# A two-layer decoder on one core: passes of the identity at stage ends and in front of the expert lists

## The chip, the cores and the metric

The kernel runs on one core of a Trainium2 chip. The metric is the device time of one execution in microseconds; lower is better. The program is one launch. Its engines are TensorE (PE; its weight loads are shown as PEld), VectorE (DVE), ScalarE (ACT), GpSimd (POOL) and SyncE (SP), which mainly issues DMA transfers.

## What is computed

The reference is a decoder of two layers over 8 sequences of 112 tokens with width 512, and a context of 375 tokens per sequence:

```
x += self_attention_0(layernorm(x))          # 16 heads, tril mask times scores
x += cross_attention_0(layernorm(x), ctx)    # 16 heads, int8 fake quantisation
x += ffn_0(layernorm(x))                     # rms, rope attention (32 query, 8 kv heads of 64),
                                             # rms, top 4 of 16 experts: (silu(h w1) * (h w3)) w2
x += self_attention_1(layernorm(x))          # 16 heads, low-rank additions to each projection
x += joint_attention_1(layernorm(x), ctx)    # 16 query heads, 4 kv heads of 128, rope
x += experts_1(layernorm(x))                 # top 6 of 16 experts, plus shared ones
```

All data are float32.

## The kernel before, in words

The program is a row of twelve stages, each with its own semaphores and PSUM tile of eight banks: front, self0, cross1, p2, self2, r2c4, the expert stage e2, self3, p4, joint4, s5 and the expert stage e5. At the end of each, `Stage.__exit__` frees its semaphores and puts a barrier of all engines (lines L82 and L84). Each engine drains, reports, and goes on when all have; the slowest engine sets the time.

Most stages are a `Segment`. It holds parts (a projection, an attention, an output product), and each part has one program per engine, written as a generator. `run(order)` walks a hand-made list of part names on every engine, and so sets in which order the parts' steps stand in each queue (`play`). The parts that matter here:

- `ContextPart` in front makes keys and values of the context. It multiplies into banks 0 to 3 for keys and 4 to 6 for values (L133), and DVE evacuates them (L2870, L2874). Its semaphore k_ready counts the evacuated key blocks, 4 per batch.
- `SelfAttentionPart` makes scores (L1498), a softmax on DVE, POOL and ACT (L1527, L1531, L1474, L1565), transposes (L1487, L1670 in the cross attention) and products with the values (L1511). `CrossAttentionPart` has scores at L1682 and value products at L1695. These operands are plain float32; scores of one head use 32, 64 or 128 rows.
- Most projections (L133, L1362) split each operand into a high and a low float32r part and multiply three times.
- `RopeQkvPart` in p2 and p4 makes queries, keys and values in banks 0 to 5.

`routed_expert_stage` (e2 and e5) works through a list of items of 128 token rows for one expert. For an item, DVE makes a one-hot matrix (L856), PE turns it into a list of tokens (L910, L912), DVE forms indices (L835, L839), POOL gathers the rows from DRAM by an indirect DMA (L734), PE transposes them (L920), ACT and DVE split them (L778, L844), and PE multiplies by the expert's weights (L876 to L878). The result is weighted, transposed (L886; L942 at the end), multiplied again and added to DRAM by POOL (L745). All engines read table words into registers first (L677, L596). The weights of the first expert are loaded in the stage before; ACT and DVE split them (L760, L807, L813). In DVE's queue the first list's index steps stand ahead of the split L807.

Line L82 is where the profile puts the drains of a stage end. The identity, `core.ident`, is a float32 tile of 128 x 128 that the transposes use too.

Of the kernel before, what the change touches and what calls it, by code (L numbers as in the profile page):

```python
# [63 lines left out]
class Stage:  # L64
# [36 lines left out]

    def block(self):
        return self.ctx.enter_context(self.nc.Block()) if self.shared is None else self.shared.block


class Order:
# [495 lines left out]
def routed_expert_stage(core, name, routing, w_up, w_down, chunks, h_rows, acc, raw, next_raw=()):  # L602
# [6 lines left out]
    with Stage(core, name) as s:  # L609
# [259 lines left out]

        @block.tensor  # L870
        def _(pe):
            pe.wait_ge(made, n_made)

            def split_product(out, lhs, rhs, k, n_k):

                pe.matmul(out, lhs[0], rhs[0], start=k == 0, stop=False)  # L876
                pe.matmul(out, lhs[0], rhs[1], start=False, stop=False)  # L877
                return pe.matmul(out, lhs[1], rhs[0], start=False, stop=k == n_k - 1)  # L878

            def tick(j, u, item, now):  # L880
                i = item(-1)
                if i is not None:
                    pe.wait_ge(act_ready, i + 1)
                    reuse(pe, a_ready, i)
                    for c in range(n_c):
                        last = pe.transpose(ps[0:chunks[c], A_BANK, c * 128:(c + 1) * 128], act_raw[:, offs[c]:offs[c] + chunks[c]],  # L886
                                            core.ident[:, :])
                    last.then_inc(a_transposed, 1)
                i = item(0)
                if i is not None:  # L890
                    e, which = now.e, now.which
                    slot = e % 2
                    pe.wait_ge(h_ready, i + 1)
                    reuse(pe, act_ready, i - 1)

                    with pe.If(which != TT):
                        for k in range(KC):
                            pe.wait_ge(up_ready, e * KC + k + 1)
                            for part in range(2):
                                cols = slice(part * hid, (part + 1) * hid)  # L900
                                last = split_product(ps[:, 2 * (u % 2) + part, 0:hid], (hT[0][u % 2][:, k, :], hT[1][u % 2][:, k, :]),
                                                     [w[:, bass.ds(slot * KC + k, 1), cols] for w in (up_hi, up_lo)], k, KC)
                        last.then_inc(gu_done, 1)
                    with pe.If(which == TT):
                        pe.matmul(ps[:, 2 * (u % 2), 0:2], hT[1][u % 2][:, 0, :], hT[1][u % 2][:, 0, 0:2], start=True, stop=True).then_inc(gu_done, 1)
                i = item(2)
                if i is not None:
                    pe.wait_ge(onehot_ready, i + 1)
                    reuse(pe, idx_ready, i)
                    pe.matmul(ps[:, LIST_BANK, 0:3], id_bf[:, :], spare_no[:, :], start=True, stop=False)  # L910
                    for m in range(TT):
                        last = pe.matmul(ps[:, LIST_BANK, 0:3], onehot[:, u % 2, m, :], token_no[:, m, :], start=False, stop=m == TT - 1)  # L912
                    last.then_inc(listed, 1)
                i = item(1)
                if i is not None:
                    v = (u + 1) % 4
                    pe.wait_ge(gathered[v % 2], landed(i, v % 2))
                    reuse(pe, h_ready, i)
                    for c in range(KC):
                        last = pe.transpose(ps[:, H_BANK, c * 128:(c + 1) * 128], rows[:, v, c * 128:(c + 1) * 128], core.ident[:, :])  # L920
                    last.then_inc(h_transposed, 1)
                i = item(-1)
                if i is not None:
                    e, which = now.e_before, now.which_before
                    slot = e % 2
                    pe.wait_ge(a_ready, i + 1)
                    reuse(pe, y_ready, i)

                    with pe.If(which != TT):
                        pe.wait_ge(dn_ready, (e + 1) * n_dn)  # L930
                        for k in range(n_c):
                            last = split_product(ps[:, Y_BANK, :], [t[0:chunks[k], k, :] for t in aT],
                                                 [w[0:chunks[k], bass.ds(slot * n_c + k, 1), :] for w in (dn_hi, dn_lo)], k, n_c)
                        last.then_inc(y_done, 1)
                    with pe.If(which == TT):
                        pe.matmul(ps[:, Y_BANK, 0:2], aT[0][:, 0, :], aT[0][:, 0, 0:2], start=True, stop=True).then_inc(y_done, 1)
            n_used = run(pe, tick)
            j = n_used // 2 * 2
            pe.wait_ge(act_ready, j + 2)
            pe.wait_ge(a_ready, j + 1)  # L940
            for c in range(n_c):
                last = pe.transpose(ps[0:chunks[c], A_BANK, c * 128:(c + 1) * 128], act_raw[:, offs[c]:offs[c] + chunks[c]], core.ident[:, :])  # L942
            last.then_inc(a_transposed, 1)


class Segment(Stage):
# [18 lines left out]
            for _ in rest:  # L965
                pass

    def run(self, order):
        block = self.ctx.enter_context(self.nc.Block())

        @block.sync
        def _(sp):
            self.play(sp, "sync", order)

        @block.gpsimd
        def _(pool):
            self.play(pool, "gpsimd", order)

        @block.vector
        def _(dve):  # L980
            self.play(dve, "vector", order)

        @block.scalar
        def _(act):
            self.play(act, "scalar", order)

        @block.tensor
        def _(pe):
            self.play(pe, "tensor", order)


class RopeQkvPart:
# [1753 lines left out]
class ContextPart:  # L2746


    def __init__(self, g, name, wk, wv, k_to, v_to, biases, k_banks, v_banks):
# [15 lines left out]
        c_ready = g.sems(f"{name}_c_ready", 2)  # L2765
        b_in, first_c_in, hi_ready, c_hi_ready, padded, k_mm, v_mm, k_ready, v_ready = (
            g.sem(f"{name}_{n}") for n in ("b_in", "first_c_in", "hi_ready", "c_hi_ready", "padded", "k_mm", "v_mm", "k_ready", "v_ready"))
        self.steps = 1 + B * KC

        def values(b, n):  # L2770

# [331 lines left out]
def decoder(nc, ins, out, blocks=range(6), debug_x=None):  # L3103

    with ExitStack() as ctx:
# [24 lines left out]
        if True:  # L3130
            with ExitStack() as held:
                wq = held.enter_context(nc.sbuf_tensor("x0_wq", [128, KC, D], F32R))
                q_scale = held.enter_context(nc.sbuf_tensor("x0_q_scale", [128, KC], F32))
                with Segment(core, "front") as g:
                    c = ContextPart(g, "c1", "L0_xattn_wk", "L0_xattn_wv", k_ctx, v_ctx, ("L0_xattn_bk", "L0_xattn_bv"),
                                    k_banks=(0, 1, 2, 3), v_banks=(4, 5, 6))
                    n = FirstNormPart(g, "n0", (7,), late=1)
                    w, wq_tmp = c.w_raw[:, 0, :, :], c.w_raw[:, 1, :, :]
                    first = QuantWeightPart(g, "w1q", "L0_xattn_wq", w, wq_tmp, lambda sp: sp.wait_ge(c.w_ready[0], KC),
                                            lambda dve: dve.wait_ge(c.w_ready[1], KC), wq, 7,  # L3140
                                            lambda pe: pe.wait_ge(n.t_free, B), scale=q_scale)
                    second = QuantWeightPart(g, "w1p", "L0_xattn_wp", w, wq_tmp, lambda sp: sp.wait_ge(first.wq_ready, KC),
                                             lambda dve: dve.wait_ge(first.t_done, KC), wp_hi, 7,
                                             lambda pe: pe.wait_ge(first.done, KC), lo=wp_lo)
                    order = ["c1", "n0"] + ["c1"] * 4 + ["c1", "n0"] * (n.steps - 1)
                    order += ["w1q"] + ["c1", "w1q", "w1q"] * 7 + ["w1p"] + ["c1", "w1p", "w1p"] * 5 + ["c1", "w1p"] * 5
                    f = FirstWeightPart(g, "f", ins["L0_attn_Wq"], first_hi, first_lo)
                    g.run(order[:24] + ["f"] + order[24:-30] + [n for name in order[-30:-25] for n in (name, "f")] + order[-25:])
                others = held.enter_context(nc.sbuf_tensor("x1_others", [128, 4, KC, D], F32R))
                flat = others[:, :, :, :].bitcast(F32).rearrange("p a k d -> p (a k d)")  # L3150
                n_q, n_k, n_v = 2 * 4 * T, 2 * 4 * C, 2 * CCH * (D + 96)
# [3 lines left out]
                with Segment(core, "self0") as g:  # L3155
# [11 lines left out]
                    order = ["x"] + self_attention_order(p, a, o, then.steps)  # L3167
                    keys_at = len(order) - order[::-1].index("p") + 4
                    queries_at = [i for i, n in enumerate(order) if n == "then"][5]
                    g.run(order[:keys_at] + ["x"] + order[keys_at:queries_at] + ["x"] + order[queries_at:])  # L3170
                with Segment(core, "cross1") as g:
                    a = CrossAttentionPart(g, "a", 32, lambda b: q1[b], lambda b: [(slice(0, C), k_ctx[b])],
                                           lambda b: [v_ctx[b, c, 0:CT, :] for c in range(CCH)], [CT] * CCH, 32.0 ** -0.5,
# [7 lines left out]
        with hold_h0:  # L3181
            with ExitStack() as inner:
                cos_t = inner.enter_context(nc.sbuf_tensor("f0_cos", [128, TT, 2, 32], F32))
                sin_t = inner.enter_context(nc.sbuf_tensor("f0_sin", [128, TT, 2, 32], F32))
                with Segment(core, "p2") as g:
# [9 lines left out]
                        [(v2[:, 0, 0:8 * 65].rearrange("p (h e) -> p h e", e=65)[:, :, 0:64], v_all[tokens_of(0), :].rearrange("t (h d) -> t h d", d=64))]],  # L3195
                        ones=v2)
                    order = ["p"] * 4 + ["p", "t", "t"] * (t.steps // 2)
                    g.run(f.placed(order + ["t"] * (t.steps - order.count("t")) + ["p"] * (p.steps - order.count("p"))))
            with Segment(core, "self2") as g:
                wo = [g.sb(f"wo_{part}", [128, 16, D], F32R) for part in ("hi", "lo")]  # L3200
                a = SelfAttentionPart(g, "a", *own_qkv(64, 32, 0.125, (0, 1), (2, 3), (4, 5), "causal", ALU.add), tiles=(q2, k2, v2))
# [42 lines left out]
        if 4 in blocks:  # L3244
# [4 lines left out]
            with Segment(core, "p4") as g:  # L3249
# [7 lines left out]
                    [(k4[:, 0, :, C:C + T], k_all[:, tokens_of(0)].rearrange("(c p) t -> p c t", p=128))] +  # L3257
                    [(v4[0:CT, 0, c, :], v_ctx[0, c, 0:CT, :]) for c in range(CCH)],
                    [(v4[0:T, 0, CCH, :], v_all[tokens_of(0), :])]])
                g.run(f.placed(["p"] * p.steps))  # L3260
            with Segment(core, "joint4") as g:
                wo = [g.sb(f"wo_{part}", [128, 16, D], F32R) for part in ("hi", "lo")]
                a = CrossAttentionPart(g, "a", 128, lambda b: q_all[:, tokens_of(b)],
# [117 lines left out]
```

## Time and profile before

| | us |
|---|---|
| median of 3 runs (lowest, highest) | 2848.71 (2846.34, 2851.26) |
| the profiled execution, own time | 2851.77 |
| its span, first to last instruction | 2850.1 |
| PE busy in the span | 2607.6 (91%) |
| PEld, DVE, ACT, POOL busy | 2146.5, 1713.2, 1131.1, 774.3 |

The span is that of one execution; the 1.7 us between it and the execution's own time lie before and behind it. Busy matmuls overlap, so a busy PE is not PE at its peak. TensorE's clock is granted by the chip at one of two levels, 1.2 or 2.4 GHz; the profile gives the granted clock of a stretch as a share of the upper one.

### The profile page before, as it was taken

Reading aid. Unit: us, or ns where it says so; the run is one execution under the profiler, and the core shown is the slowest. Engines: PE = TensorE matmul, PEld = TensorE weight load, DVE = VectorE, ACT = ScalarE, POOL = GpSimd, SP = SyncE. Lnnn points to the kernel's source line nnn. Section 1 sums busy time; section 2 is a strip of 40 time slices with the busy share of each in tenths; the row PEclk is TensorE's granted clock in tenths of the full one; section 3 lists DMA queues with packets and bytes.
Section 4 is the critical chain, followed back from the end, with each engine's and each line's share of the span. In section 5 each row is a group of like instructions: output and inputs, shape, how many; then the busy total and the mean of one; then the engine's idle time right before and its main releaser. Section 6 shows DMA issues by size and latency. Waiting matters only on the chain. (4 is left out here: it accounts for less than half of the span.)

```text
span 2850.1 us, 50284 instructions
## 1 busy us (share of the span) xinstructions
PE 2607.6 (91%) x15563; PEld 2146.5 (75%) x15564; DVE 1713.2 (60%) x3341; ACT 1131.1 (40%) x2434; POOL 774.3 (27%) x792
## 2 busy tenths in 40 slices
PE   8999799979899999699996998999999999799997
PEld 7888677768688777588774786767777788688886
DVE  4537657769777566567664466865444426566564
ACT  2113256523343234455452133755544421444342
POOL 3213100024233235322332100740000012355554
PEclk9999899999899989899997899999999989899998
DMA  5453122125521045477773432344222031566663
GB/s 188 153 145 97 34 81 72 44 80 164 174 74 54 28 143 179 141 215 211 206 206 77 109 76 76 115 138 130 72 62 75 19 121 60 149 162 162 156 160 66
DMA packets 289287, 333.00 MB, mean 117 GB/s; under 512 B 147446, under 2 KB 202694, under 8 KB 287313
## 3 DMA queue, kind: packets, MB, share of 16 engines
q1 hardware_dynamic: 217904, 252.57, 28.6%
q0 software_dynamic: 20640, 51.74, 9.2%
q10 hardware_dynamic: 50560, 26.34, 3.2%
q8 instruction: 106, 1.74, 0.3%
q14 instruction: 77, 0.62, 0.1%
HBM read 233.86 MB, written 96.72 MB: 116 GB/s over the span
## 5 line engine op out<-in xcount | busy, mean ns | idle before, releaser
L876 PE MATMUL e_psum<-e_up_hi,hT_hi 128*128 x672 | 246.1, 366 | 21.4 <-DVE hT_lo L844 15.1
L877 PE MATMUL e_psum<-e_up_lo,hT_hi 128*128 x672 | 238.0, 354 | 0.0
L878 PE MATMUL e_psum<-e_up_hi,hT_lo 128*128 x672 | 237.7, 354 | 0.0
L876 PEld LDWEIGHTS e_psum<-e_up_hi,hT_hi 128*128 128x128 f32 x672 | 127.6, 190 | 44.2 <-issue 31.3
L1474 POOL TENSOR_TENSOR self_a_p<-self_a_p,self_a_mx 112x448 f32<-112x448 f32 x96 | 96.1, 1001 | 206.9 <-DVE self_a_mx L1531 206.9
L773 ACT ACTIVATE e_gate<-e_psum 128x352 f32<-128x352 f32 (+1 forms) x86 | 44.5, 517 | 258.8 <-PE e_psum L878 258.4
L850 DVE TENSOR_TENSOR hT_lo<-e_psum,hT_hi 128x256 fp32r<-128x256 f32 (+2 forms) x138 | 55.6, 435 | 145.6 <-ACT hT_hi L791 145.6
L1565 ACT ACTIVATE self_a_p<-self_a_p 112x448 f32<-112x448 f32 x128 | 71.6, 574 | 168.4 <-POOL self_a_p L1474 113.0
L878 PEld LDWEIGHTS e_psum<-e_up_hi,hT_lo 128*128 128x128 f32 x672 | 127.6, 190 | 12.3
L877 PEld LDWEIGHTS e_psum<-e_up_lo,hT_hi 128*128 128x128 f32 x672 | 127.9, 190 | 10.7
L1695 PEld LDWEIGHTS joint_psum<-x_v,joint_a_pt 125*112 125x112 f32 (+1 forms) x1024 | 119.6, 178 | 19.2 <-issue 13.5
L745 POOL DMA_INDIRECT out<-e_y,e_back x51 | 124.9, 2449 | 17.2 <-issue 17.2
L807 DVE TENSOR_TENSOR e_up_lo<-e_up_raw,e_up_hi 128x1024 f32 (+3 forms) x128 | 127.6, 1050 | 2.9 <-issue 2.6
L1154 POOL TENSOR_TENSOR p_p_z<-p_p_straight,p_p_crossed 128x512 f32<-128x512 f32 x70 | 98.4, 1406 | 113.4 <-DVE p_p_crossed L1136 111.5
L1695 PE MATMUL joint_psum<-x_v,joint_a_pt 125*112 125x128 f32 (+1 forms) x1024 | 124.9, 275 | 2.9 <-ACT joint_a_pt L1740 2.8
L826 DVE SCALAR_TENSOR_TENSOR e_act_raw<-e_gate,e_rows,e_psum 128x352 f32<-128x352 f32 (+1 forms) x86 | 55.4, 644 | 120.1 <-ACT e_gate L773 118.8
L1708 DVE TENSOR_REDUCE joint_a_mx<-joint_psum 112x1 f32<-112x487 f32 x128 | 85.1, 665 | 70.5 <-PE joint_psum L1682 70.3
L876 PE MATMUL e_psum<-e_dn_hi,hT_hi 128*128 (+1 forms) x285 | 122.0, 428 | 1.3 <-issue 0.7
L1682 PE MATMUL joint_psum<-x_first,x_q 128*112 128x487 f32 x256 | 117.1, 579 | 6.0 <-PEq L85 3.8
L133 PE MATMUL p_psum<-p_p_w_hi,hT_hi 128*128 128x512 f32 x280 | 115.4, 412 | 1.9 <-DVE p_p_w_lo L1120 1.9
L760 ACT ACTIVATE e_up_hi<-e_up_raw 128x1024 f32 (+3 forms) x128 | 107.7, 923 | 20.7 <-PEq L85 20.6
L878 PE MATMUL e_psum<-e_dn_hi,hT_lo 128*128 (+1 forms) x285 | 114.4, 402 | 0.0
(559 smaller groups left out, 7380.3 us busy)
## 6 DMA issues: line engine op xcount, KB each, us to landing
e_up_raw<-in_L_ffn_w SPq DMA_DIRECT2D x64, 512.0 KB, 5.3
e_up_raw<-in_L_ffn_w SPq DMA_DIRECT2D x64, 352.0 KB, 4.5
e_dn_raw<-in_L_ffn_w SPq DMA_DIRECT2D x16, 1024.0 KB, 5.5
q_all<-p_p_t_stage ACTq DMA_DIRECT2D x56, 256.0 KB, 2.3
e_dn_raw<-in_L_ffn_w SPq DMA_DIRECT2D x16, 512.0 KB, 4.2
x_q<-q_all SPq DMA_DIRECT2D x8, 896.0 KB, 5.2
k_ctx<-front_c_t_stage SPq DMA_DIRECT2D x32, 187.5 KB, 2.6
v_ctx<-front_c_v_stage SPq DMA_DIRECT2D x24, 250.0 KB
```

Of the source, the lines that this page charges most:

```text
L133: last = pe.matmul(out, a, b, start=(k == 0 and i == 0), stop=(k == n_k - 1 and i == len(pairs) - 1))
L745: pool.indirect_dma_start(out=acc, out_offset=bass.IndirectOffsetOnAxis(ap=back[:, v, :], axis=0), in_=y[:, v, :], in_offset=None, compute ...
L760: act.activation(up_hi[:, bass.ds(slot * KC + k, 1), :], up_raw[:, k:k + 1, :], ACT.Copy).then_inc(up_hi_ready, 1)
L807: dve.tensor_tensor(up_lo[:, bass.ds(slot * KC + k, 1), :], up_raw[:, k:k + 1, :], up_hi[:, bass.ds(slot * KC + k, 1), :].bitcast(F32), AL ...
L876: pe.matmul(out, lhs[0], rhs[0], start=k == 0, stop=False)
L877: pe.matmul(out, lhs[0], rhs[1], start=False, stop=False)
L878: return pe.matmul(out, lhs[1], rhs[0], start=False, stop=k == n_k - 1)
L1154: both = pool.tensor_tensor(z[:, r, :], straight[:, r, :], crossed[:, r, :], ALU.add)
L1474: pool.tensor_tensor(p[:, i % RING, :, :], p[:, i % RING, :, :], mx[:, i % RING, :].unsqueeze(2).to_broadcast([T, group, T]), ALU.subtract ...
L1682: pe.matmul(ps[0:T, s_banks[i % N_S], 0:S], q[rows_of(h), b % 2, h // row_groups, :], k[rows_of(kv_of(h)), b % 2, kv_of(h) // row_groups, ...
L1695: last = pe.matmul(ps[0:T, o_banks[group % N_O], col:col + 128], pt[0:n, w % PT, c, :], v[0:n, b % 2, c, first:first + 128], start=(c == 0 ...
L1708: dve.tensor_reduce(mx[:, r, :], ps[0:T, s_banks[i % N_S], 0:S], AX.X, ALU.max).then_inc(mx_ready, 1)
```

## The change

A helper, `keep_busy`, issues plain float32 matmuls of the identity by the identity, 128 columns each, into a bank that nobody reads afterwards. Each starts and ends its own accumulation. It is called in eight places:

| where | bank | passes | waits for |
|---|---|---|---|
| end of front | 0 | 18 | the last batch's first key block evacuated |
| end of self0 | 4 | 18 | - |
| end of p2 | 7 | 36 | - |
| end of p4 | 7 | 18 | - |
| end of e2, end of e5 | 0 | 48 each | - |
| start of e2, start of e5, ahead of the wait for POOL's constants | 6 | 18 each | - |

No other instruction is moved or changed, on any engine; no stage gets another buffer.

```diff
+def keep_busy(pe, core, ps, bank, passes, evacuated=None):
+
+    if evacuated is not None:
+        pe.wait_ge(*evacuated)
+    for _ in range(passes):
+        pe.matmul(ps[:, bank, 0:128], core.ident[:, :], core.ident[:, :], start=True, stop=True)
...
         @block.tensor
         def _(pe):
+            keep_busy(pe, core, ps, Y_BANK, 18)
             pe.wait_ge(made, n_made)
...
             last.then_inc(a_transposed, 1)
+            keep_busy(pe, core, ps, 0, 48)
...
-    def run(self, order):
+    def run(self, order, kept_busy=None):
...
             self.play(pe, "tensor", order)
+            if kept_busy:
+                keep_busy(pe, self.core, self.ps, *kept_busy)
...
-                    g.run(order[:24] + ["f"] + order[24:-30] + [n for name in order[-30:-25] for n in (name, "f")] + order[-25:])
+                    g.run(order[:24] + ["f"] + order[24:-30] + [n for name in order[-30:-25] for n in (name, "f")] + order[-25:], (0, 18, (c.k_ready, (B - 1) * KC + 1)))
...
-                    g.run(order[:keys_at] + ["x"] + order[keys_at:queries_at] + ["x"] + order[queries_at:])
+                    g.run(order[:keys_at] + ["x"] + order[keys_at:queries_at] + ["x"] + order[queries_at:], (4, 18))
...
-                    g.run(f.placed(order + ["t"] * (t.steps - order.count("t")) + ["p"] * (p.steps - order.count("p"))))
+                    g.run(f.placed(order + ["t"] * (t.steps - order.count("t")) + ["p"] * (p.steps - order.count("p"))), (7, 36))
...
-                g.run(f.placed(["p"] * p.steps))
+                g.run(f.placed(["p"] * p.steps), (7, 18))
```

PE's queue at the end of p2 and the start of self2, before (p_psum is p2's PSUM tile, hT the normed tokens; the two branches are the barrier and the next block):

```order
L133 MATMUL p_psum<-p_p_w_hi,hT_hi 128x512
L133 MATMUL p_psum<-p_p_w_lo,hT_hi 128x512
L133 MATMUL p_psum<-p_p_w_hi,hT_lo 128x512
L82 UNCONDITIONAL_BRANCH
L987 UNCONDITIONAL_BRANCH
L1498 MATMUL self_psum<-x_first_hi,x_wp_hi 112x112 x16
L1487 MATMUL self_psum<-ident,self_a_p 112x112 x8
```

The same place with the change (its lines are numbered a little higher):

```order
L141 MATMUL p_psum<-p_p_w_hi,hT_hi 128x512
L141 MATMUL p_psum<-p_p_w_lo,hT_hi 128x512
L141 MATMUL p_psum<-p_p_w_hi,hT_lo 128x512
L111 MATMUL p_psum<-ident 128x128 x36
L82 UNCONDITIONAL_BRANCH
L997 UNCONDITIONAL_BRANCH
L1510 MATMUL self_psum<-x_first_hi,x_wp_hi 112x112 x16
```

The 36 passes stand between the last projection and the barrier, in front of self2's scores.

PE's queue at the start of e2, before (the loads and ISA rows read table words into registers):

```order
L82 UNCONDITIONAL_BRANCH
L870 UNCONDITIONAL_BRANCH
L677 TENSOR_LOAD r_ticks
L677 ISA x2
L596 TENSOR_LOAD r_ticks
L596 ISA x2
L596 TENSOR_LOAD r_ticks
L596 ISA x2
L910 MATMUL e_psum<-e_spare_no,e_id_bf 128x3
L912 MATMUL e_psum<-e_token_no,e_onehot 128x3 x7
```

And with the change:

```order
L82 UNCONDITIONAL_BRANCH
L878 UNCONDITIONAL_BRANCH
L111 MATMUL e_psum<-ident 128x128 x18
L685 TENSOR_LOAD r_ticks
L685 ISA x2
L604 TENSOR_LOAD r_ticks
L604 ISA x2
L604 TENSOR_LOAD r_ticks
L604 ISA x2
L919 MATMUL e_psum<-e_spare_no,e_id_bf 128x3
L921 MATMUL e_psum<-e_token_no,e_onehot 128x3 x7
```

The 18 passes stand behind the barrier and ahead of everything that PE does for the first list.

## Rows read from the trace of the kernel before

**Rows 1.** The page, part 2: TensorE's granted clock in 40 slices, in tenths of full speed.

```profile
PEclk9999899999899989899997899999999989899998
```

**Rows 2.** Busy by stretch: us; PE, PEld, DVE, ACT, POOL; granted clock, DMA, GB/s.

```profile
161.80:165.20 3.40, 3.40 (x10) 3.02 (x11) 0.00 (x0) 0.00 (x0) 1.16 (x2) 0.51 0.56 124
341.30:346.10 4.80, 4.80 (x13) 4.28 (x14) 0.74 (x1) 0.00 (x0) 0.00 (x0) 0.50 0.00 0
354.90:366.90 12.00, 10.52 (x38) 6.81 (x40) 3.93 (x12) 5.24 (x16) 0.03 (x1) 0.51 0.55 180
749.70:766.00 16.30, 13.29 (x90) 11.90 (x92) 9.53 (x17) 7.86 (x13) 5.60 (x6) 0.50 0.63 167
772.90:776.40 3.50, 3.43 (x17) 3.44 (x18) 3.43 (x6) 2.35 (x5) 1.13 (x2) 0.52 1.15 330
1186.80:1190.70 3.90, 0.00 (x0) 0.00 (x0) 1.09 (x1) 3.90 (x5) 0.79 (x9) 0.50 0.53 140
1199.40:1202.90 3.50, 3.50 (x8) 2.79 (x9) 2.50 (x2) 0.00 (x0) 0.00 (x0) 0.50 0.92 349
1546.30:1571.40 25.10, 14.66 (x42) 10.97 (x43) 13.52 (x32) 4.69 (x8) 9.41 (x11) 0.50 0.36 111
1920.10:1923.10 3.00, 3.00 (x4) 1.35 (x5) 0.82 (x2) 0.15 (x1) 0.05 (x1) 0.50 0.64 178
```

**Rows 3.** Lines L82 (stage end) and L942: count, ns min/median/max, first and last start.

```profile
L82 SPq DRAIN  x1: 7/7/7, 160.7 to 160.7; - x1
...
L82 SPq DRAIN  x1: 7/7/7, 353.8 to 353.8; - x1
...
L82 SPq DRAIN  x1: 7/7/7, 748.8 to 748.8; - x1
...
L82 POOLq DRAIN  x1: 5942/5942/5942, 1537.0 to 1537.0; - x1
...
L82 SPq DRAIN  x1: 7/7/7, 1919.3 to 1919.3; - x1
...
L82 POOLq DRAIN  x1: 5786/5786/5786, 2843.4 to 2843.4; - x1
...
L942 PE MATMUL e_psum<-ident,e_act_raw x3: 415/417/417, 2837.1 to 2837.5; 128*128 128x128 f32 x2, 128*96 128x128 f32 x1
```

**Rows 4.** Timeline: first PE rows of five stages; start, us, in brackets idle before.

```profile
161.77 0.63 PE L1362 MATMUL self_psum<-hT_hi,x_first_hi 128*128 128x448 f32 x1 [4.57 <-PEq L85]
...
354.87 1.60 PE L1682 MATMUL cross_psum<-x_others 32*112 32x375 f32 x6 [4.54 <-PEq L85]
...
749.64 1.84 PE L1498 MATMUL self_psum<-x_first_hi,x_wp_hi 64*112 64x112 f32 x16 [6.94 <-PEq L85]
...
1546.22 0.79 PE L133 MATMUL self_psum<-self_p_lora_hi 16*128 16x512 f32 x1 [14.87 <-DVE self_p_lora_lo L1289]
...
1920.09 5.00 PE L1682 MATMUL joint_psum<-x_first,x_q 128*112 128x487 f32 x8 [3.81 <-PEq L85]
```

**Rows 5.** Page, part 5, and timeline: plain f32 products with 128 columns.

```profile
L1695 PE MATMUL joint_psum<-x_v,joint_a_pt 125*112 125x128 f32 (+1 forms) x1024 | 124.9, 275 | 2.9 <-ACT joint_a_pt L1740 2.8
...
766.89 1.92 PE L1511 MATMUL self_psum<-x_first_lo,self_a_pt 112*112 112x128 f32 x16
```

**Rows 6.** Timeline of self2's start.

```profile
753.42 1.84 PE L1498 MATMUL self_psum<-x_first_hi,x_wp_hi 64*112 64x112 f32 x16 [1.94 <-DVE self_a_p L1527]
...
753.88 0.58 ACT L1565 ACTIVATE self_a_p<-self_a_p 112x448 f32<-112x448 f32 x1 [3.00 <-POOL self_a_p L1474]
...
755.19 1.74 PE L1487 MATMUL self_psum<-ident,self_a_p 112*112 112x112 f32 x8
```

**Rows 7.** Timeline of the first expert stage's start.

```profile
1186.77 3.89 ACT L760 ACTIVATE e_up_hi<-e_up_raw 128x1024 fp32r<-128x1024 f32 x4 [4.11 <-PEq L85]
...
1190.71 0.19 PE L910 MATMUL e_psum<-e_spare_no,e_id_bf 128*128 128x3 bf16 x1 [8.67 <-DVE e_onehot L856]
...
1196.22 1.11 PE L920 MATMUL e_psum<-ident,e_rows 128*128 128x128 f32 x4 [3.03 <-DMA e_rows<-h_rows,e_idx]
```

More of the change, by code:

```diff
@@ L2767, in __init__ @@
             g.sem(f"{name}_{n}") for n in ("b_in", "first_c_in", "hi_ready", "c_hi_ready", "padded", "k_mm", "v_mm", "k_ready", "v_ready"))
-        self.steps = 1 + B * KC
+        self.steps, self.k_ready = 1 + B * KC, k_ready
         def values(b, n):
```

## The prediction

> **What bounds the kernel now.** I read the page first, then busy time by stretch of time, then the ends and starts of the stages, because the added passes run only there. The page's second part has TensorE's granted clock in 40 slices [rows 1]: nearly full everywhere, down to 0.8 in a few slices. Of the two levels, 1.2 and 2.4 GHz, the low one is 0.5. Busy time by stretch shows where it was granted while TensorE (PE) had work [rows 2]. The reader is to see four stage starts: 3.4 us of self0 at 0.51, 12.0 us of cross1, 16.3 us of self2 and 3.0 us of joint4, with PE busy for 3.40, 10.52, 13.29 and 3.00 us of them. Self3's first 25 us and the first products of an expert stage are low too. In such a stretch each matmul takes twice as long, so half of PE's busy time there could come back, where PE is what the stage waits for.
>
> The drains at the stage ends [rows 3] say what a passing engine may use up. PE is done first; the barrier waits for the last DMA to land on SP (160.7, 353.8, 748.8, 1919.3) or for POOL's drain of 5.94 and 5.79 us (to 1542.9 and 2849.2). The first PE rows of the next stages, with the idle time in front of them [rows 4], give PE's own end: 161.77 less 4.57 is 157.20, and likewise 350.33, 742.70 and 1916.28. PE starts some 1.1 us behind SP's drain. A clock that was still 2.4 GHz when the work ended is low after 3.81 us without work (1920.09) as after 4.57.
>
> **The price of a pass.** The trace has no identity pass. The nearest row is the plain f32 product with 128 columns [rows 5]. The joint stage makes 8 x 16 x 4 = 512 of them and has 1024 records, so one call is two records. Sixteen records take 1.92 us at the high clock; less the 0.275 us of the last one, that is 0.110 us each. A pass is 0.22 us at the high clock and 0.44 us at the low one. So 18 passes are 4.0 us or 7.9 us, 36 are 7.9 us, and 48 are 10.6 us or 21.1 us. All passes together are 8 places and 222 calls, 49 us of PE time, and almost all of it lies in time that was idle.
>
> **End of the front stage, 18 passes.** Their wait is for an evacuation of bank 0 three blocks back in DVE's order: free. They run from 157.2 to 161.2; SP was done at 160.7, so the next stage starts 0.5 us later. It then starts at the high clock and gets back half of 3.40 us. Net 1.2 us gained; bounds 0.5 lost and 2.9 gained, the upper one by a cold start twice as long.
>
> **End of self0, 18 passes.** 350.3 to 354.3 against 353.8: 0.5 us later. Upper bound of the gain: half of 10.52, so 4.8 net. Lower bound: 0.5 lost. PE's work there is thin once it is fast: the first scores (1.60 us), a wait for the softmax, scores and transposes. Since thin work lets the clock fall in the middle of self2 too (it is 0.52 again from 772.9 [rows 2], though rows from 766.89 run at the high clock [rows 5]), I count only the first scores and what follows up to the first transposes, 1.9 us, and take 1.4 net.
>
> **End of p2, 36 passes.** 742.7 to 750.6 against 748.8: self2 starts 1.8 us later. Its first scores fall from 1.84 to 1.04 us. The first transposes wait [rows 6] for ScalarE's exponential, which begins at 753.88 and takes 0.58, or for PE, which frees at 755.19. Moved by 1.8 less 0.8, ScalarE ends at 755.5. So PE is 0.3 us behind before where it was, and between the two score groups it still waits some 1.9 us. I take 0.3 lost; bounds 1.8 lost and 4.8 gained (half of 13.29 less 1.8).
>
> **End of p4, 18 passes.** 1916.3 to 1920.2 against 1919.3: 0.9 us later, and half of 3.00 us back, in a stage where PE streams its scores without a gap. Net 0.6 gained; bounds 0.9 lost and 1.5 gained.
>
> **Ends of the expert stages, 48 passes.** 1531.35 to 1541.9; POOL's drain hides them by 1.0 us. Self3's first PE work is at 1546.22, so 4.3 us stay idle, more than the 3.81 us that was enough before joint4. The clock falls again: no gain, no cost. Bounds: 7.3 gained (half of 14.66), 1 lost if the passes start at the low clock. At the program's end the last transposes are done at 2837.9 [rows 3], and 10.6 more make 2848.5, against 2849.2: nothing, or 1.3 lost by the same low start.
>
> **In front of the first list, 18 passes, twice.** Here nothing has kept the clock up: it is 0.50 from 1186.8 on [rows 2]. The engines enter at 1186.8 [rows 7], and the first list ran at 1190.71, when DVE's one-hot was there. It heads a chain: list, indices, gather, transposes at 1196.22 (released by the gather's DMA), split, products from 1199.4 on [rows 2]. Weights are split behind the index steps in DVE's order, so they move with it. What is late in the list is late in the stage. The register loads in front of the list go to the sequencer beside the passes. Steady work has raised the clock after 3.4, 3.5 and 4.8 us at the low level [rows 2]; I take 4.1. Then 9.3 passes are cold and 8.7 warm: 4.1 + 1.9 = 6.0 us, the list at 1192.8, 2.1 us late. The other expert stage runs the same function; also 2.1. Bounds each: 4.0 lost (all cold, 7.9 us) and 2.2 gained (passes at the high clock, and the clock kept for the 1.11 us of transposes and 3.5 us of products). I do not count on it, for PE waits over 5 us on the gather again.
>
> How long the cold part lasts varies. "TensorE: Matmul & The Clock Gate" in the Trainium skill, Part 1, says that the count of cold matmuls in one kernel differs between runs (it names 6, 11 and 14). By that rule this term has a spread of its own; the trace agrees, with 8, 10 and 13 records in the three rows [rows 2].
>
> **The sum.** 1.2 + 1.4 - 0.3 + 0.6 + 0 + 0 - 2.1 - 2.1 = -1.3, so 1.3 us slower. The profiled execution took 2851.8 us (span 2850.1), 3.1 over the median of the runs, 2848.7. On the median that makes 2850.0. A measurement of this kernel can tell about 0.2%, 5.7 us, from no change: 2843.0 to 2854.4.
>
> **Rivals.**
> - *The clock is held into the stages.* If thin work at the start of cross1 and self2 is enough once the clock is up, the terms become 1.2 + 4.8 + 4.8 + 0.6 - 4.2 = 7.2 gained: 2841.5. For it: PE is busy 10.52 of 12.0 us there, and both stages are PE's for most of their length. Against it: the busy share is halved at the high clock, and the softmax chain sets the first groups.
> - *The first list pays in full.* The two rows of passes in front of the list stay cold to the end, 4.0 us late each, and the products behind the gather find a cold clock for 4.8 us, not 3.5 (0.65 each): 2.9 - 8.0 - 1.3 = 6.4 lost, 2855.1. It decides from 1.45 us of delay per list, where the 2.9 us of the stage ends are used up. For it: idle and low at 1186.8. Against it: steady rows raised the clock within 4.8 us.
> - *The change does not hold the clock at all.* Then the starts are later by 3.7 in sum, the lists by 8.0, and 48 cold passes overrun both of POOL's drains by 9.5 us and more: about 31 lost, near 2880. Against it: self2's clock, low until 766.0 [rows 2], is high at 766.89 [rows 5], behind nothing but f32 products and transposes.
>
> The page named above, Part 4, says that transposes do not raise the clock as matmuls do. The passes are plain matmuls with the identity on both sides; if they counted like transposes, the third rival would be the result, and the stretch before 766.0, in which transposes [rows 6] share PE with products while the clock comes up, speaks against a strict form of it.
>
> **How the numbers follow.** My forecast 0.56, with all terms within their middle: same. The held clock 0.22: faster. The list 0.18 and no hold 0.04: slower. The low end takes in the held clock (2841.5) and half a microsecond more; the high end takes in the list (2855.1) and the 1.3 to 2 us of a cold start at the program's end. What is left out is the third rival and the far ends: 2841 to 2857.
>
> **What would show it.** Right: granted clock 1.0 in the first 3 us of self0 and joint4; the first PE row of self2 about 1.8 us further behind the last real matmul of p2 than 6.94; two records of 0.11 us per pass; the list of e2 starting about 6 us behind the barrier, not 4. Self3 at 0.50 as before. Wrong: the first list on time, so that the passes ran at the high clock; cross1 or self2 at 1.0 over their first 12 us; or PE the last engine at the program's end.

## The result, and the profile after

| | before | with the change |
|---|---|---|
| median of 20 runs each (lowest, highest), us | 2850.18 (2841.49, 2853.55) | 2854.95 (2847.12, 2861.43) |
| ratio, 95% interval | | 1.0022 [1.0014, 1.003] |
| the profiled execution, us | 2851.77 | 2852.24 |
| its span, us | 2850.1 | 2850.6 |
| PE busy, us | 2607.6 | 2653.7 |

The change costs 4.8 us by the medians, 0.17%. The ratio comes from all runs and not from the two medians: it says 0.22%, 6.3 us, with an interval from 4.0 to 8.6. Either is about the bound of 0.2% below which the forecast called two times the same. The forecast was 2850.0 with a range to 2857, and its upper bound for "the same" was 2854.4. The two profiled executions are 0.5 us apart only, so one pair of traces can't hold the whole loss; why is taken up below. The page of the changed kernel, parts 1 and 2:

```profile
PE 2653.7 (93%) x16007; PEld 2193.7 (77%) x16008; DVE 1712.6 (60%) x3341; ACT 1129.9 (40%) x2434; POOL 775.4 (27%) x792
...
PEclk9999999999999989899998899999999989899999
```

The 16007 records are 444 more than before: 222 passes, two records each. The clock row [rows 1] has risen by a tenth in four slices and fallen in none, while the time went up. A row that looks better is no gain in itself. Busy time by stretch, the changed kernel, the answer to [rows 2] (columns: stretch; us; PE, PEld, DVE, ACT, POOL busy with records; granted clock, DMA share, GB/s):

```profile
161.80:165.20 3.40, 2.73 (x14) 2.57 (x15) 0.00 (x0) 0.00 (x0) 1.23 (x2) 1.00 0.44 74
355.20:358.60 3.40, 1.92 (x10) 0.76 (x11) 2.04 (x7) 1.76 (x6) 0.04 (x1) 1.00 0.58 147
358.80:365.80 7.00, 7.00 (x31) 5.23 (x29) 1.69 (x6) 3.52 (x10) 0.00 (x0) 0.51 0.57 202
750.60:754.80 4.20, 1.64 (x28) 1.46 (x30) 2.39 (x4) 1.38 (x2) 0.98 (x2) 1.00 0.52 149
754.80:765.10 10.30, 9.40 (x58) 8.16 (x54) 6.58 (x13) 5.59 (x10) 4.66 (x5) 0.50 0.80 204
1199.70:1205.40 5.70, 5.67 (x13) 4.46 (x14) 2.45 (x2) 0.00 (x0) 0.00 (x0) 0.50 0.82 276
1546.70:1570.60 23.90, 13.46 (x39) 9.92 (x40) 13.24 (x31) 4.69 (x8) 9.41 (x11) 0.50 0.42 117
1923.60:1926.60 3.00, 2.90 (x7) 1.17 (x8) 1.60 (x4) 1.00 (x3) 0.03 (x1) 1.00 0.67 191
```

Self0 and joint4 now start at the high clock and keep it. Cross1 and self2 start at the high clock and lose it after 3 to 4 us, with PE busy for 1.92 of 3.40 us and 1.64 of 4.20 us; then they run low for 7.0 and 10.3 us, where the whole low stretch had been 12.0 and 16.3. The first products of e2 run low for 5.7 us, 3.5 before. Self3 starts low as before.

The stage end of p2 in the changed kernel (line L82 in one window: count, ns min/median/max, first and last start), and behind it the timeline of PE there:

```profile
L82 PEldq DRAIN  x1: 2175/2175/2175, 747.6 to 747.6; - x1
L82 SPq DRAIN  x1: 7/7/7, 748.4 to 748.4; - x1
L82 SPq EVENT_SEMAPHORE  x1: 17/17/17, 749.9 to 749.9; - x1
```
```profile
741.52 8.20 PE L111 MATMUL p_psum<-ident 128*128 128x128 f32 x72
750.59 1.04 PE L1510 MATMUL self_psum<-x_first_hi,x_wp_hi 64*112 64x112 f32 x16 [0.87 <-PEq L85]
```

SP is done at 748.4 and now waits for PE, until 749.9; before, PE waited for SP [rows 3]. The idle time in front of self2's first row is 0.87 us instead of 6.94 [rows 4].

The starts of the two expert stages in the changed kernel (timeline; the first list is L919, the gathered rows' transposes L929, the first product L885):

```profile
1185.24 5.72 PE L111 MATMUL e_psum<-ident 128*128 128x128 f32 x36 [4.47 <-PEq L85]
1188.01 1.09 DVE L864 TENSOR_TENSOR e_onehot<-r_pos,r_place_no 128x896 bf16 x1 [10.26 <-issue]
1191.14 0.18 PE L919 MATMUL e_psum<-e_spare_no,e_id_bf 128*128 128x3 bf16 x1 [0.18 <-issue]
...
1191.54 0.16 DVE L843 TENSOR_REDUCE e_small<-e_psum 128x1 f32<-128x2 f32 x1 [2.44 <-PE e_psum L921]
...
1196.48 1.12 PE L929 MATMUL e_psum<-ident,e_rows 128*128 128x128 f32 x4 [2.88 <-DMA e_rows<-h_rows,e_idx]
...
1199.73 0.79 PE L885 MATMUL e_psum<-e_up_hi,hT_hi 128*128 x1 [2.13 <-DVE hT_lo L852]
...
2428.70 6.87 PE L111 MATMUL e_psum<-ident 128*128 128x128 f32 x36 [3.91 <-PEq L85]
...
2435.41 0.17 PE L919 MATMUL e_psum<-e_spare_no,e_id_bf 128*128 128x3 bf16 x1
...
2443.97 0.65 PE L885 MATMUL e_psum<-e_up_hi,hT_hi 128*128 x1 [2.02 <-DVE hT_lo L852]
```

In e2 the one-hot is ready at 1189.1 and the list runs at 1191.14, right behind the passes: 5.90 us behind the passes' start, where it had been 3.94 behind the entry [rows 7]. DVE stands 2.44 us idle for it, where it had been 0.47 (the row of L835 at 1191.12). The first product comes 14.5 us behind the entry instead of 12.6. In e5 the list is 6.71 us behind the entry; there it had been 3.68, and the first product comes at 15.3 instead of 12.3, by these rows of the kernel before:

```profile
2425.96 2.83 ACT L760 ACTIVATE e_up_hi<-e_up_raw 128x704 fp32r<-128x704 f32 x4 [16.47 <-PEq L85]
...
2429.64 0.19 PE L910 MATMUL e_psum<-e_spare_no,e_id_bf 128*128 128x3 bf16 x1 [7.58 <-DVE e_onehot L856]
...
2438.25 0.66 PE L876 MATMUL e_psum<-e_up_hi,hT_hi 128*128 x1 [2.02 <-DVE hT_lo L844]
```

### The profile page after: what moved, and what is told of

Its sections match the earlier page's. It is cut to its first block and busy times, and to the rows that moved or that the text cites. A ratio compares the mean times of both kernels' runs of the same rounds, so it can differ in the third digit from the quotient of the medians.

```text
span 2850.6 us, 51172 instructions
## 1 busy us (share of the span) xinstructions
PE 2653.7 (93%) x16007; PEld 2193.7 (77%) x16008; DVE 1712.6 (60%) x3341; ACT 1129.9 (40%) x2434; POOL 775.4 (27%) x792
## 5 line engine op out<-in xcount | busy, mean ns | idle before, releaser
L885 PE MATMUL e_psum<-e_up_hi,hT_hi 128*128 x672 | 246.6, 367 | 20.0 <-DVE hT_lo L852 13.6
L885 PEld LDWEIGHTS e_psum<-e_up_hi,hT_hi 128*128 128x128 f32 x672 | 127.9, 190 | 42.9 <-issue 30.4
L753 POOL DMA_INDIRECT out<-e_y,e_back x51 | 125.8, 2466 | 16.9 <-issue 16.9
L885 PE MATMUL e_psum<-e_dn_hi,hT_hi 128*128 (+1 forms) x285 | 121.6, 427 | 0.9 <-issue 0.2
## 6 DMA issues: line engine op xcount, KB each, us to landing
e_dn_raw<-in_L_ffn_w SPq DMA_DIRECT2D x16, 1024.0 KB, 16.3
```

What stands on the lines that cost most here:

```text
L753: pool.indirect_dma_start(out=acc, out_offset=bass.IndirectOffsetOnAxis(ap=back[:, v, :], axis=0), in_=y[:, v, :], in_offset=None, compute ...
```

## The experiments

All kernels compute the whole reference. The edits shown are on the changed kernel; in the runs that put passes in front of or behind the lists, or at p2's end alone, every place that is not named has none. Each comparison is with runs of the kernel before on the same chip. The first three take the change apart by place; the others change how many passes stand at a place, and where.

**The four segment ends alone.** Front, self0, p2 and p4 keep their passes; nothing in front of the lists, nothing at the expert stages' ends.

```diff
         def _(pe):
-            keep_busy(pe, core, ps, Y_BANK, 18)
             pe.wait_ge(made, n_made)
...
-            keep_busy(pe, core, ps, 0, 48)
```

> Only the passes at the ends of front, self0, p2 and p4. Theory 'list' (what costs is the passes in front of the first lists): the stage ends return their barrier delays, so 1 to 4 us faster than before, near 2847.5; the self2 stage 2 us shorter, the p2 stage 2 us longer, granted clock 1.0 in the first 3 us of self0, cross1, self2 and joint4. Theory 'barrier' (what costs is the barriers that these passes make late, 0.7 + 2.0 + 1.2 us in the trace of the change): 2 to 4 us slower than before, as the whole change. Theory 'expert end': no difference or slightly faster.

Measured: 2850.30 against 2850.72, ratio 0.9999 [0.999, 1.0007]. No gain and no loss that the runs can tell; the interval leaves room for 2.9 us gained or 2.0 lost.

**The passes in front of the first lists alone.** The counts of the other six places are taken out.

> Only the 18 passes in front of the two first lists. Theory 'list': each list starts 2 to 3 us later behind the stage's entry (5.7 to 6.9 us instead of 3.9 and 3.7), and the whole delay arrives at the end: 4 to 6 us slower than before, near 2855. Theory 'barrier' or 'expert end': the passes hide behind the weight splits or return their time with a warmer clock: within 1 us of before.

Measured: 2856.18 against 2850.72, ratio 1.0023 [1.0012, 1.0034]: 5.5 us slower, within the intervals as much as the whole change.

**The 48 passes at the expert stages' ends alone.**

> Only the 48 passes at the ends of the two expert stages. Theory 'list' and 'barrier': hidden behind POOL's drain of 5.9 us, clock low again in self3: within 1 us of before. Theory 'expert end': the 1.9 us by which self3 is longer in the trace of the change come from here: about 2 us slower or more.

Measured: 2849.93 against 2850.72, ratio 1.0 [0.9991, 1.0009]: nothing. In this run's e2 the last pass ends 1.2 us before the stage's semaphore clear, in time for POOL's drain. In the changed kernel's e2 the drain lasts to 1537.22 + 5.94 = 1543.16, and the last pass ends at 1543.4, 0.2 us behind it.

The three parts add to -0.4 + 5.5 - 0.8 = +4.3 us; the change measured +4.8. By its interval each part is uncertain by 2.5 to 3 us.

**36 passes in front of the first lists instead of 18, and no others.** A dose test: if PE's queue is what the list waits for, 18 more passes cost their own length in each expert stage.

```diff
-            keep_busy(pe, core, ps, Y_BANK, 18)
+            keep_busy(pe, core, ps, Y_BANK, 36)
```

> 36 passes in front of each first list, no others. Theory 'list': the 18 additional ones run at the high clock (0.22 us each), so each list is 4.0 us later than with 18: 8 us slower than the kernel with 18, 12 to 14 us slower than before. If the time in front of the list is hidden somewhere behind (weights, the DVE queue), less than half of that.

Measured: 2864.61 against 2850.72, ratio 1.0045 [1.0031, 1.006]. That is 13.9 us, 8.4 more than 18 passes; 2 x 18 passes at 0.22 us are 7.9. Its timeline has the list at the end of the row of passes again:

```profile
1188.03 9.78 PE L111 MATMUL e_psum<-ident 128*128 128x128 f32 x72 [5.22 <-PEq L85]
1197.91 0.18 PE L919 MATMUL e_psum<-e_spare_no,e_id_bf 128*128 128x3 bf16 x1
```

**9 passes in front of the first lists, and no others.**

```diff
-            keep_busy(pe, core, ps, Y_BANK, 18)
+            keep_busy(pe, core, ps, Y_BANK, 9)
```

> 9 passes in front of each first list instead of 18, no others. Nine cold passes take 9 x 0.44 = 3.9 us, as long as PE waits there for DVE's one-hot in any case. Theory 'list' (the cost is only what the passes overrun this wait by): no difference to before, within 1 us; first list 3.7 to 3.9 us behind PE's entry. Rival (passes there cost by something else, such as keeping PE's queue or the register loads busy): half of the 5.5 us that 18 passes cost.

Measured: 2851.01 against 2850.35, ratio 0.9998 [0.9988, 1.0009]. Nine fit in front of the one-hot at the low clock (3.91 us for 18 records, list at 3.92 behind the entry), and they cost nothing. They bring nothing either: the gather leaves PE idle behind them.

**Passes where PE waits, not where DVE waits for PE.** Eight in front of the list; three behind the first list, six behind the second, and four behind the first transposes, each behind the signal to DVE or ACT. No others.

```diff
-            keep_busy(pe, core, ps, Y_BANK, 18)
+            keep_busy(pe, core, ps, Y_BANK, 8)
...
                     last.then_inc(listed, 1)
+                    if isinstance(j, int) and j in (-2, -1):
+                        keep_busy(pe, core, ps, Y_BANK, 3 if j == -2 else 6)
...
                     last.then_inc(h_transposed, 1)
+                    if isinstance(j, int) and j == -1:
+                        keep_busy(pe, core, ps, Y_BANK, 4)
```

> The passes of the expert starts are laid into waits that PE has anyhow: 8 ahead of the first list, 3 between the first two lists, 6 while the gather is under way, 4 while the first rows are split. No others. Theory 'list': the lists start on time, and the first products, 3.5 and 3.75 us of them cold before, run at the high clock: up to 1.9 us gained per expert stage, 2 to 4 us in sum, near 2847.5. Rival (the clock falls all the same, or the first products are not what the stage waits for): within 1 us of before.

Measured: 2848.09 against 2850.35, ratio 0.9991 [0.9982, 1.0]. 2.3 us faster by the medians; the interval touches no change.

**Fewer passes at the four segment ends** (15, 17, 29, 13), so that PE ends with SP and not behind it; no others.

```diff
-... (0, 18, (c.k_ready, (B - 1) * KC + 1)))
+... (0, 15, (c.k_ready, (B - 1) * KC + 1)))
-... (4, 18))
+... (4, 17))
-... (7, 36))
+... (7, 29))
-... (7, 18))
+... (7, 13))
```

> The four segment ends with fewer passes, so that PE is done before the last transfer: 15, 17, 29 and 13 instead of 18, 18, 36 and 18. Theory 'the barrier delays eat the warm starts': barriers on time (front 161.1, p2 143.8, p4 151.7 us) and the warm starts kept (cross1 1.4, self2 2.1 us shorter): 3 to 4 us faster than before and than with the full counts, near 2847. Rival: with 1 to 2 us idle left in front of the next stage the clock falls in some executions and the gain is lost: within 1 us of before.

Measured: 2846.24 against 2850.35, ratio 0.9987 [0.9978, 0.9997]. The time came as expected, but not all of it by the expected path: cross1 is not 1.4 us shorter in this kernel (the stage times below).

**Both: fewer passes at the ends, and the passes behind the lists.**

> Both together: the trimmed counts at four stage ends and the passes laid into the waits of the expert starts. The two gains lie in different stages and add: 5 to 8 us faster than before, near 2844, if both theories hold; less than 2 us if neither does.

Measured: 2843.44 (2840.46 to 2854.96, 12 runs) against 2850.35, ratio 0.9977 [0.9967, 0.9987]. This beats both kernels: 6.9 us under before. Busy time by stretch of this kernel, at e2's entry, behind the second list, and at the first products:

```profile
1182.40:1185.80 3.40, 3.38 (x16) 3.18 (x16) 0.66 (x1) 3.40 (x4) 0.76 (x9) 0.58 0.50 113
1188.60:1191.50 2.90, 2.85 (x18) 2.55 (x14) 2.90 (x3) 0.00 (x0) 0.70 (x1) 0.51 0.51 138
1195.20:1198.70 3.50, 3.50 (x15) 2.86 (x16) 2.52 (x2) 0.00 (x0) 0.00 (x0) 1.00 0.84 319
```

The passes behind the second list run low, and the products behind them start at the high clock. That is what the change wanted from its 18 passes in front of the list, and here no one waits for them: the first list runs 3.9 us behind the entry as before.

**The four ends and the fewer passes, both again, side by side.**

> The four segment ends alone (18, 18, 36, 18 passes), a second time and beside the trimmed counts on one chip. If the counts themselves matter (barriers 4.6 us later in sum by the trace of the change, against 0.8 in the trimmed kernel), this is within 0.05% of before and 2 to 4 us above the trimmed kernel. If the earlier difference was scatter, both lie within 1 us of each other.

> The trimmed counts (15, 17, 29, 13) again. Counts matter: 2847 to 2848 where before is 2850.5, so 0.9988 with an interval below 1. Scatter: 2849.5 to 2850.5.

Measured: 2849.46 and 2844.90 against 2849.41; ratios 0.9998 [0.9989, 1.0007] and 0.9987 [0.9978, 0.9996]. Both results stood. Side by side the fewer passes are 4.6 us below the full counts.

**The end of p2 alone, with 36 and with 29 passes.**

> Only the 36 passes at p2's end. By the trace of the change the barrier is 2.0 us later and self2 2.1 us shorter: no difference, 2850.4 +- 1. The forecast's term said 0.3 lost, the held-clock rival 4.8 gained (2845.7).

> Only 29 passes at p2's end. Barrier 0.4 us later and self2 still 2.1 shorter: 1.7 us gained, 2848.8. If the clock falls within the shorter row, self2 is as long as before and this equals before.

Measured: 2852.48 and 2851.89 against 2849.41; ratios 1.0018 [1.0009, 1.0027] and 1.0009 [1.0, 1.0018]. Both expectations missed: alone, this place loses 3.1 us by the medians with 36 passes (5.1 by the ratio) and 2.5 with 29, where the interval touches no change. The trace shows a wait that no one had counted. The first mask of self2's softmax is loaded by SP at the stage's start. The same DVE row before, in the changed kernel, and with 36 passes at p2's end alone, one fence each:

```profile
751.55 0.62 DVE L1527 TENSOR_TENSOR self_a_p<-self_psum,self_a_mask 112x448 f32<-112x448 f32 x1 [5.00 <-PE self_psum L1498]
```
```profile
752.33 0.62 DVE L1539 TENSOR_TENSOR self_a_p<-self_psum,self_a_mask 112x448 f32<-112x448 f32 x1 [6.20 <-DMA self_a_mask<-in_causal]
```
```profile
751.68 1.04 PE L1508 MATMUL self_psum<-x_first_hi,x_wp_hi 64*112 64x112 f32 x16 [0.87 <-PEq L85]
...
754.77 0.62 DVE L1537 TENSOR_TENSOR self_a_p<-self_psum,self_a_mask 112x448 f32<-112x448 f32 x1 [8.55 <-DMA self_a_mask<-in_causal]
...
756.63 1.84 PE L1508 MATMUL self_psum<-x_first_hi,x_wp_hi 64*112 64x112 f32 x16 [3.91 <-DVE self_a_p L1537]
```

Before, the cold scores (1.84 us) ended just behind the mask's landing, 1.8 us from issue, and PE released DVE. With warm scores (1.04 us) the mask is the last to come, 1.74 us behind the first score in the changed kernel and 3.09 with p2's end alone (it lands 3.1 us from its issue there, and 3.5 with 29 passes). By then the clock has fallen: the second group of scores takes 1.84 us again, and the low stretch behind it is 13.5 us long with PE busy for 11.69. Busy time by stretch of that kernel:

```profile
751.70:755.80 4.10, 1.02 (x16) 0.84 (x16) 1.00 (x2) 1.22 (x1) 0.04 (x1) 1.00 0.51 140
755.90:769.40 13.50, 11.69 (x76) 10.57 (x78) 8.43 (x16) 6.86 (x12) 5.60 (x6) 0.50 0.59 156
```

**Stage times of the profiled executions.** From one stage's semaphore clear (L84) to the next, in us:

| stage | before | the change | ends | ends again | fewer | fewer again | p2 alone, 36 |
|---|---|---|---|---|---|---|---|
| self0 | 193.1 | 192.7 | 193.5 | 192.6 | 192.3 | 193.7 | 193.1 |
| cross1 | 251.2 | 249.8 | 249.7 | 249.8 | 251.2 | 251.1 | 251.0 |
| p2 | 143.8 | 145.9 | 145.9 | 145.9 | 145.6 | 145.6 | 145.9 |
| self2 | 242.0 | 240.0 | 239.9 | 240.0 | 239.9 | 239.7 | 243.7 |
| e2 | 357.1 | 359.1 | 357.5 | 357.4 | 355.6 | 355.3 | 355.9 |
| self3 | 224.6 | 226.4 | 224.8 | 225.6 | 223.7 | 223.6 | 226.0 |
| p4 | 151.7 | 152.9 | 153.0 | 152.7 | 151.2 | 152.1 | 152.1 |
| joint4 | 392.1 | 391.5 | 391.8 | 392.4 | 391.9 | 392.0 | 391.7 |
| e5 | 424.1 | 421.9 | 422.2 | 426.1 | 422.6 | 423.1 | 422.2 |

With the full counts p2 is 2.1 us longer and self2 2.0 shorter; cross1 gives back 1.4. The table also shows what one execution can't carry. E5 takes 422.2 to 426.1 us where nothing in it was changed, and self3 from 223.6 to 226.0. Self0 takes 193.1 us in the profiled execution of the kernel before and in two others without passes at front's end, but 194.8 to 195.4 in the remaining five, so the column "before" is not the usual one there. In the changed kernel e5 is 2.2 shorter than before although its first product comes 3.0 later, which is the main reason why the two profiled executions differ by 0.5 us only. The medians, not this pair, carry the verdict.

**One stretch that does not scatter.** In e2 the time from the semaphore clear in front of it to the end of PE's last matmul that is not a pass separates the kernels in one execution each. What scatters in e2 is the tail behind that matmul, 8.5 to 12.0 us, in which POOL adds the last results to DRAM and drains.

| passes at e2's start | executions | us to the end of PE's last matmul |
|---|---|---|
| none | 8 | 344.9 to 345.5 |
| 9 in front of the list | 1 | 345.6 |
| 18 in front (the change; the lists alone) | 2 | 348.0, 348.8 |
| 36 in front | 1 | 351.9 |
| 8 in front and 13 behind the signals | 2 | 343.6, 343.5 |

So 18 passes cost e2 some 3 us, and passes placed behind the signals gain 1.3 to 2.0. The same measure scatters by 5 us in e5 (409.5 to 414.6 without passes) and can't be used there.

**Where full and fewer passes differ.** The stage table hides two differences, since they cancel against the barriers. With 15 passes at front's end and 17 at self0's, cross1 is as long as before (251.2 and 251.1), with 18 and 18 it is 1.4 us shorter; with the passes behind the lists as well it was 248.1, in the one execution at hand. And p2, which has no passes in front of it, starts slower with fewer passes: its first products run low for over 5.3 us instead of 3.2, and its last real matmul ends 1.3 us later behind the stage's clear (138.7 to 138.8 us in the three executions with fewer passes at the ends, 137.4 to 137.5 in the other eleven). Busy time by stretch, the changed kernel and then the one with fewer passes:

```profile
604.80:608.00 3.20, 3.17 (x8) 2.52 (x9) 0.00 (x0) 0.00 (x0) 0.00 (x0) 0.50 0.63 182
608.10:611.80 3.70, 3.70 (x18) 3.06 (x17) 1.29 (x2) 0.00 (x0) 0.89 (x1) 1.00 0.78 274
```
```profile
606.20:611.50 5.30, 5.27 (x13) 4.14 (x14) 0.00 (x0) 0.00 (x0) 0.00 (x0) 0.50 0.65 212
611.90:613.20 1.30, 1.30 (x7) 1.07 (x6) 1.19 (x2) 0.00 (x0) 0.03 (x1) 0.99 0.99 372
```

## Why the prediction was right, and where it wasn't

The time fell in the range, on the slow side of the forecast: +4.8 us measured (+6.3 by the ratio), +1.3 forecast. The sign was right, and so was the place that costs. The size was not: 2854.95 lies 0.15 us from the rival "the first list pays in full" (2855.1, chance 0.18) and just above the 2854.4 up to which the forecast of 0.56 reached, and only the wide range covers it. Some 1.5 us of the distance are no fault of the sum, for the median of the kernel before went from 2848.7 to 2850.2 with more runs. By its steps:

- *A pass is two records of 0.11 us, 0.22 in all.* Right: 72 records took 8.20 us at p2's end, less 0.275 for the last is 0.110 each.
- *The barriers are 0.5, 0.5, 1.8 and 0.9 us later.* From the last real matmul to the semaphore clear it took 3.86, 3.82, 6.41 and 3.29 us before and 4.42, 4.81, 8.39 and 4.36 in the changed kernel: 0.6, 1.0, 2.0 and 1.1 later, 4.6 for 3.7 in sum. With the fewer passes it is 0.8 in sum in one execution and 1.0 in the other.
- *The stages behind them gain 6.6 us in sum at their starts* (1.7, 1.9, 1.5 and 1.5; less the 3.7 of the barriers that is 2.9 net). Too much. By the stage table self0, cross1, self2 and joint4 are 0.4, 1.4, 2.0 and 0.6 shorter in the changed kernel; self0's 0.4 holds its own end's 1.0 us of delay, so its start gained 1.4, and the sum is 5.4. Net of 4.6 that is 0.8 and not 2.9, less than stages scatter, and the runs of the ends alone show no gain either (0.9999 and 0.9998). The direction in cross1 and self2 was as argued: a clock that is high at the start falls within the first 5 us of the stage, in which PE waits for the softmax.
- *Self2's first scores fall from 1.84 to 1.04 us, and the softmax moves by that.* The scores did, the softmax didn't. Measured from the stage's clear, ScalarE's first exponential ends at 5.17 us (754.66 + 0.58 - 750.07) where it ended at 5.34 (753.88 + 0.58 - 749.12): 0.17 earlier, not 0.8. The 2.0 us that self2 gains all the same come later: its low stretch ends 15.0 us behind the clear (765.1) and not 16.9 (766.0). What the step left out is the mask's DMA, which was hidden by 0.1 us of cold scores. Forecast and rivals asked only what PE, DVE and ScalarE do; the wait that took over was for SP's load.
- *The ends of the expert stages: nothing.* Right, twice over: 1.0 [0.9991, 1.0009] alone, and self3's start at 0.50. In the changed kernel's e2, though, the passes ended 0.2 us behind POOL's drain and not 1.0 us ahead of it.
- *Each first list is 2.1 us late and the stage with it.* This is the term that was mis-sized. The list was 2.0 us late in e2, as worked out, and 3.0 in e5; the other execution, of the lists alone, has the rows of passes at 5.72 and 5.88 us. In e2 the products behind it also stayed cold for 5.7 us instead of 3.5, which at half speed is 1.1 more; the forecast had no term for that. The 2.8 and 3.6 us by which e2's last matmul is later with 18 passes are about the sum of the two. The runs put both lists at 5.5 us, where the forecast had 4.2. The rival "the first list pays in full" gave 2855.1 and named the price of its decision, 1.45 us per list. In its number it came truest, in part by luck: the passes did not stay cold to their end (5.7 to 6.9 us for 18, not 7.9), and the stage ends gave nothing where that rival had left them 2.9.
- *The held clock.* Its 2841.5 came from no thing that happened: the clock fell in cross1 and self2. *No hold at all* is excluded by the 1.00 at self0 and joint4.
- *The clock is low after 3.81 us without work.* Not always. With 36 passes in front of the lists and none at p4's end, joint4 began at the high clock behind the same idle time; in the other seven executions without these passes its first row was at the low one. The row and its stretch:

```profile
1926.92 2.27 PE L1693 MATMUL joint_psum<-x_first,x_q 128*112 128x487 f32 x5 [3.80 <-PEq L85]
...
1926.90:1929.90 3.00, 2.88 (x7) 1.17 (x8) 1.60 (x4) 0.95 (x3) 0.08 (x1) 1.00 0.59 186
```

"TensorE: Matmul & The Clock Gate" in the Trainium skill, Part 1, says that the number of matmuls which run at the low clock varies from run to run. The traces agree: the 18 passes in front of e5's list took 6.87 us in the changed kernel and 5.88 in the one with the lists alone.

What is shown: the loss sits in front of the first lists (alone +5.5; doubled +13.9; halved nothing; e2's last matmul 3 us later in two executions), and passes behind the signals turn it into a gain in e2. The stage ends with the full counts are neutral within 3 us. What is not: why fewer passes at the ends gain 4 us. That gain was measured twice. The barriers come 3.8 us earlier with them, but cross1 gives back 1.4 less and p2's start costs 1.3, which leaves 1.1. The other visible difference is in e2, 2 us, and 1.5 of it lie in the tail behind PE's last matmul (10.5 and 10.4 us against 12.0 and 12.0); that tail was 10.2 to 10.7 in five other executions with other edits too, so it can't be put down to the counts. Nor was it found why the mask lands 1.3 us later with p2's end alone, with the same instructions at that place. The ends of front, self0 and p4 were not tried each by itself.

## What to carry to other kernels

Passes that hold the clock are free only where PE waits anyway, and only as many as that wait is long at the clock they will really run at: nine in front of the list were free, 18 were not. What overruns the wait in front of the first instruction of a chain (list, gather, product) is paid in full, and at the low clock each pass costs twice. Behind the last signal that another engine waits for there is more room. Before a stage start is made faster on one engine, look for the transfer that lands just in time now: its cover is what is taken away. For an effect of 0.1% compare a stretch that doesn't scatter, as e2 up to its last matmul, and not the whole of one execution.

## What had not been expected

- With a few passes fewer at the ends of front and self0 cross1 gained nothing in two of three executions, and all three had a slower start of p2, a stage later. Why is not shown.
- A place can be worth less alone than with others: p2's end alone is 3 us slower (1.0018), and with the three other ends the sum is 0. The two executions with p2's end alone are also the two with the late mask; whether that is their doing is not shown.
- A 49 KB mask, the first transfer that SP issues in the stage, landed 1.7 to 1.8 us from its issue in seven of nine executions looked at and 3.1 and 3.5 us in the other two.
- A clock can stay high over 3.8 us without work, as in front of joint4 in one of eight executions.
